# Residual of one pair of sequences transposed by VectorE blocks and transfers instead of TensorE, in a two-layer kernel on one core

## The reference

```python
def _L0_cond_ref(x, ...):
    attn = softmax((x @ Wq) @ (x @ Wk).T * V ** -0.5)          # per sequence
    attn_out = attn @ (x @ Wv) @ Wp + bp
    cms_out = gelu(attn_out @ cW1 + cb1) @ cW2 + cb2 + one_hot(target_codes)
    modifier = gelu(concat([attn_out, cms_out]) @ mW1 + mb1) @ mW2 + mb2
    return clip(x + cms_out + modifier, 0.0, 1.0)

def _L1_cond_ref(stream, hidden_states, W_down, b_down, W_up, b_up, ln_w, ln_b):
    h = gelu(hidden_states @ W_down[stream] + b_down[stream])
    h = h @ W_up[stream] + b_up[stream]
    h = hidden_states + h                                       # the residual
    mean = jnp.mean(h, axis=-1, keepdims=True)
    var = jnp.mean(jnp.square(h - mean), axis=-1, keepdims=True)
    h = (h - mean) * jax.lax.rsqrt(var + LN_EPS)
    return h * ln_w[stream][:, None, :] + ln_b[stream][:, None, :]
```

## Time and profile before

| | |
|---|---|
| median of 3 runs | 1032.73 us (1032.29 to 1033.24) |
| the profiled execution | 1032.2 us, of which span 1030.4 us |
| PE busy | 1023.4 us, 99% of the span, granted clock 0.999 |
| DVE busy | 795.0 us, 77% |
| ACT busy | 524.8 us, 51% |
| POOL busy | 26.5 us, 3% |
| DMA | 103.71 MB, mean 101 GB/s |

### The profile page before, as it was taken

The page is one execution under the profiler, slowest core; times in us unless marked ns, Lnnn a source line. Parts: engine busy times, 40 slices in busy tenths (PEclk is TensorE's granted clock), DMA queues, the critical chain, the costliest instruction groups (busy, mean ns, idle before and its releaser), DMA issues.

```text
span 1030.4 us, 13832 instructions
## 1 busy us (share of the span) xinstructions
PE 1023.4 (99%) x4834; PEld 858.0 (83%) x4834; DVE 795.0 (77%) x1364; ACT 524.8 (51%) x954; POOL 26.5 (3%) x42
## 2 busy tenths in 40 slices
PE   9999999999999999999999999999999999999997
PEld 8899888888888888888889888888888888888886
DVE  5657857767598898887966896677668889887798
ACT  4337864444265443433565587454435644434357
POOL 0000000000000021000000000000000001200001
PEclk9999999999999999999999999999999999999999
DMA  9351311210143272621643312312004322423142
GB/s 209 61 205 39 102 42 49 74 41 21 62 157 118 93 201 86 166 80 54 239 118 109 116 62 82 123 42 82 21 21 163 143 85 100 162 101 107 42 164 82
DMA packets 108558, 103.71 MB, mean 101 GB/s; under 512 B 54254, under 2 KB 89418, under 8 KB 104650
## 3 DMA queue, kind: packets, MB, share of 16 engines
q1 hardware_dynamic: 108400, 102.81, 30.9%
q10 hardware_dynamic: 90, 0.02, 0.0%
HBM read 79.74 MB, written 20.97 MB: 98 GB/s over the span
## 4 chain that ended last, share of the span: by engine, by line
PE 96%; DVE 2%; ACT 1%; issue 0%; DVEq 0%; ACTq 0%
PE bank L231 31%; PE bank L232 31%; PE bank L233 31%; PE bank L270 1%; PE bank L259 1%; DVE z_last L1315 0%; DVE z_last L1326 0%; PE bank L473 0%; PE bank L246 0%; ACT gel L857 0%; DVE xp2l L1043 0%; DVE xp3l L1043 0%; ACT e3h L601 0%; ACT h33h L856 0%; ACT h32h L856 0%
## 5 line engine op out<-in xcount | busy, mean ns | idle before, releaser
L693 ACT ACTIVATE sbc<-sbc,bias 128x512 f32<-128x512 f32 x112 | 80.5, 724 | 234.1 <-DVE sbc L1134 170.0
L231 PE MATMUL bank<-hid_hi,w_lo 128*128 128x512 f32 x512 | 199.7, 390 | 0.0
L233 PE MATMUL bank<-hid_lo,w_hi 128*128 128x512 f32 x512 | 199.3, 389 | 0.0
L232 PE MATMUL bank<-hid_hi,w_hi 128*128 128x512 f32 x512 | 199.2, 389 | 0.0
L1159 DVE TENSOR_TENSOR acc<-bank,acc 128x512 f32<-128x512 f32 x224 | 153.7, 686 | 51.4 <-PE bank L233 51.0
L231 PE MATMUL bank<-ta_hi,w_lo 128*128 128x512 f32 x448 | 174.5, 390 | 0.0
L232 PE MATMUL bank<-ta_hi,w_hi 128*128 128x512 f32 x448 | 174.3, 389 | 0.0
L233 PE MATMUL bank<-ta_lo,w_hi 128*128 128x512 f32 x448 | 174.3, 389 | 0.0
L1134 DVE TENSOR_TENSOR sbc<-bank,sbc 128x512 f32<-128x512 f32 x144 | 97.9, 686 | 41.3 <-PE bank L233 40.9
L1043 DVE TENSOR_TENSOR w_lo<-w_raw,w_hi 128x256 fp32r<-128x256 f32 (+1 forms) x176 | 99.4, 594 | 36.8 <-ACT w_hi L601 36.7
L601 ACT ACTIVATE sbc<-bank 128x512 f32<-128x512 f32 x112 | 66.2, 593 | 114.3 <-PE bank L233 112.4
(11 more groups left out here) (223 smaller groups left out, 1537.8 us busy)
## 6 DMA issues: line engine op xcount, KB each, us to landing
w_raw<-in_L_cond_mW SPq DMA_DIRECT2D x48, 512.0 KB, 3.4
w_raw<-in_L_cond_cW SPq DMA_DIRECT2D x32, 512.0 KB, 4.3
pre_d<-sbc SPq DMA_DIRECT2D x10, 1024.0 KB, 3.9
sbc<-pre_d SPq DMA_DIRECT2D x10, 1024.0 KB, 7.5
x_blk<-in_x SPq DMA_DIRECT2D x64, 64.0 KB, 2.3
e_raw<-in_L_cond_W_down SPq DMA_DIRECT2D x8, 512.0 KB, 4.6
e_raw<-in_L_cond_W_up SPq DMA_DIRECT2D x8, 512.0 KB, 4.1
proj_hi<-aw_hi SPq DMA_DIRECT2D x2, 1024.0 KB, 10.1
```

Source lines behind the costliest of these rows:

```text
L231: nc.tensor.matmul(dst, w_l, a_h, start=start, stop=False, **kw)
L232: nc.tensor.matmul(dst, w_h, a_h, start=False, stop=False, **kw)
L233: return nc.tensor.matmul(dst, w_h, a_l, start=False, stop=stop, **kw)
L693: nc.scalar.activation(dst, dst, ACT.Gelu, **kw).then_inc(g_done[key], 1)
```

## The change

In the norm of pair 1 alone the residual no longer goes through PE. DVE transposes 32x32 blocks of `acc` into `res_blk` (four instructions, after the softmax of pair 2), and sixteen transfers, four after each value tile of pair 2 on ACT's own queue, put the blocks in place in `res`. PE's up-projection starts its banks afresh, and its wait for the values' low parts (`v_l`) moves from the transposes to it. DVE adds bank and `res` into `acc`; mean and sum of squares are taken by ACT from there, with an output nobody reads (`hjunk`), and DVE and POOL do the rest tile by tile instead of half by half. ACT goes on to the value tiles of pair 3 only when all four sums are there. To free semaphores, the transfers of each of the last three column tiles of Wq and Wk share one, so that each waits for both. The branches for probabilities transposed by PE, which no pair used, are removed. The core of the diff:

```diff
-        wq_in, wk_in, wv_in = ([sem(f"w{w}_in{t}") for t in range(KT)] for w in "qkv")
+        wq_in, wv_in = ([sem(f"w{w}_in{t}") for t in range(KT)] for w in "qv")
+        wk_in = [sem("wk_in0")] + wq_in[1:]
...
-                pe.wait_ge(landed[d], 16)
+                pe.wait_ge(landed[d], 32 if i < 2 and d else 16)
...
-                elif n == 1:
-                    pe.wait_ge(v_l, 8 + t + 1)
...
+                if n == 1:
+                    pe.wait_ge(v_l, 8 + t + 1)
...
-                               u_lo[:, s, w], False, True, skip_group_check=True)
+                               u_lo[:, s, w], n == 1 and m == 0, n != 1 or m == MT - 1, skip_group_check=True)
...
-                    token_tile(t)
+                    if n != 1:
+                        token_tile(t)
...
-            v_tiles(0, range(TT))
+            for t in range(TT):
+                v_tiles(0, (t,))
+                if b:
+                    act_move_residual(act, t)
...
                 act_exps(act, n + 1)
+                act_stats_moved(act)
...
+        def act_move_residual(act, q):
+            act.wait_ge(blk_done, 8)
+            grid = lambda tile, quarter: tile[32 * quarter:32 * quarter + 32, :].rearrange("p (x c f) -> p x c f", c=4, f=32)
+            for r in range(4):
+                act.dma_start(grid(res, r)[:, :, q, :], grid(res_blk, q)[:, :, r, :]).then_inc(res_in, 16)
+
+        def act_stats_moved(act):
+            for t in range(TT):
+                col = slice(TT + t, TT + t + 1)
+                act.wait_ge(h_done, t + 1)
+                nc.scalar.activation(hjunk[:, t, :], z_tile(1, t), ACT.Identity, scale=-1.0 / V,
+                                     accum_out=nmean[:, col]).then_inc(nmean_done, 1)
+                act.wait_ge(nmean_done, t + 1)
+                nc.scalar.activation(hjunk[:, t, :], z_tile(1, t), ACT.Square, bias=nmean[:, col],
+                                     accum_out=ssq[:, col]).then_inc(ssq_done, 1)
+            act.wait_ge(ssq_done, TT)
...
+        def dve_residual_blocks(dve):
+            dve.wait_ge(xb_done, 8)
+            for j in range(KT):
+                nc.vector.transpose(res_blk[:, j * TB:(j + 1) * TB], acc[:, j, TB:2 * TB]).then_inc(blk_done, 1)
+
+        def dve_norm_moved(dve):
+            by_feature = lambda tile: tile.rearrange("p (k e) -> p k e", e=P)
+            dve.wait_ge(z_done[0], 4)
+            dve.wait_ge(ln_in[1], 64)
+            dve.wait_ge(res_in, 256)
+            for t in range(TT):
+                dve.wait_ge(up_mm, 4 + t + 1)
+                nc.vector.tensor_tensor(by_feature(z_tile(1, t)), by_feature(ps[t][:, :]),
+                                        res[:, :].rearrange("p (k t e) -> p k t e", k=KT, t=TT)[:, :, t, :], ALU.add)\
+                    .then_inc(h_done, 1)
...
+                dve_residual_blocks(dve)
                 dve_h3(dve, n - 1)
...
-                dve_norm(dve, n - 1)
+                dve_norm_moved(dve)
```

More of the change, by code:

```diff
@@ L361, in pe_values @@
             for t in range(TT):
[L362 to L365, removed]
                 pe.wait_ge(exp_done, 4 * n + t + 1)
@@ L371, in pe_values @@
                 last.then_inc(v_mm, 1)
[L373 to L385, removed]
         def pe_attend(pe, n):
@@ L769, in act_probs_T @@
             for b in range(SEQ):
[L770 to L775 removed]
+                act.wait_ge(raw_in[i], 256 * (n // 2 + 1))
+                act_copy(by_key(pT_hi[i], b), moved(i, b)).then_inc(pT_h, 1)
         def act_ao(act, n):
@@ L1246, in dve_probs_T @@
                 dve.wait_ge(pT_h, 2 * n + b + 1)
-                if n in MOVED:
-                    sub(by_key(pT_lo[i], b), moved(i, b), by_key(pT_hi[i], b)).then_inc(pT_l, 1)
-                else:
-                    sub(pT_lo[i][:, b, :], ps[2 * i + b][:, :], pT_hi[i][:, b, :]).then_inc(pT_l, 1)
+                sub(by_key(pT_lo[i], b), moved(i, b), by_key(pT_hi[i], b)).then_inc(pT_l, 1)
         def dve_blocks_T(dve, n):
@@ L1275, in dve_h3 @@
                 sub(h3[n][1][:, m, :], gel[n][:, m, :], h3[n][0][:, m, :]).then_inc(h3_l, 1)
+        def dve_residual_blocks(dve):
[12 more added lines that the diff above has]
+                    .then_inc(h_done, 1)
+            for t in range(TT):
+                col = slice(TT + t, TT + t + 1)
+                dve.wait_ge(ssq_done, t + 1)
+                nc.vector.tensor_scalar(veps[:, t:t + 1], ssq[:, col], 1.0 / V, LN_EPS, ALU.mult, ALU.add).then_inc(ve_done, 1)
+                nc.vector.scalar_tensor_tensor(out=z_tile(1, t), in0=z_tile(1, t), scalar=nmean[:, col],
+                                               in1=ln_p[1][:, t // TS, 0, :], op0=ALU.add, op1=ALU.mult).then_inc(z_cent, 1)
+                dve.wait_ge(rstd_done, R_BASE[1] + t + 1)
+                dve.wait_ge(z_cent, 4 + t + 1)
+                nc.vector.scalar_tensor_tensor(out=z_tile(1, t), in0=z_tile(1, t), scalar=rstd[:, t:t + 1],
+                                               in1=ln_p[1][:, t // TS, 1, :], op0=ALU.mult, op1=ALU.add)\
+                    .then_inc(z_done[1], 1)
+        R_BASE = (0, 2, 6)
         def dve_norm(dve, n, halves=(0, 1)):
@@ L1304, in dve_norm @@
                         .then_inc(z_done[pp], 1)
-        R_NO = {pt: 4 * NBAT - 3 + c + 1 for c, pt in enumerate(A_STAT)}
+        R_NO = {pt: R_BASE[2] + 1 + c + 1 for c, pt in enumerate(A_STAT)}
         def dve_eps_last(dve, pp, t):
             col = slice(TT * pp + t, TT * pp + t + 1)
-            dve.wait_ge(ssq_done, A_NO[(pp, t)] + 1)
+            dve.wait_ge(ssq_done, TT + A_NO[(pp, t)] + 1)
             nc.vector.tensor_scalar(veps[:, t:t + 1], ssq[:, col], 1.0 / V, LN_EPS, ALU.mult, ALU.add).then_inc(ve_done, 1)
@@ L1682, in pool_program @@
                 if b:
-                    for n in (2 * b - 2, 2 * b - 1):
-                        pool_norm(pool, n, halves)
+                    pool_norm(pool, 2 * b - 2, halves)
+                    pool_norm(pool, 2 * b - 1, singles)
                 pool_s(pool, b)
@@ L1820, in sync_program @@
                 sp.dma_start(proj_lo[:, slot, :], aw_lo[slot][:, :].bitcast(F32)).then_inc(proj_out, 16)
-            for n in MOVED:
-                if n < 2:
-                    move_probs(sp, n)
+            for n in range(2):
+                move_probs(sp, n)
             sync_mlp(sp, 0)
```

31 lines of the change are left out of this document (12 added, 19 removed).

## The result

The changed kernel takes **1038.21 us** in the median of 4 runs (1036.78 to 1039.28), the kernel before 1032.72 us beside it. The ratio is 1.0053, with a 95% interval of 1.0041 to 1.0065: slower by 0.5%, where I had forecast 1032.2 us and given slower a chance of 0.22. The time lies outside the range too.

What follows compares the result with a forecast made beforehand. TensorE was taken as the bound: 1032.2 - 1.67 for removed transposes + 1.18 for a new wait = 1031.7 us profiled; the same -0.5 on the median 1032.73 gave 1032.2. Range 1031.0 to 1035.6.

Steps and rivals of the forecast that it cites:

- The ceiling of 1.67 us: Most the change can gain: TensorE's time for the sixteen residual transposes before the up-projection, 0.16% of the run.
- The issue step: Time from one residual transfer issue to the next on ScalarE's queue: 0.653 us, four in 2.61 us.
- Rival (d): ScalarE's issues take turns with SyncE's sixteen, at 1.31 us each; 1040.4 us, chance 0.05.
- The sum of 238 stays below: From 552 to 560 us, 138 GB/s of load plus 100 for the moves stays below 292, so issues aren't lengthened.
- Rival (c): Issues grow with the runs or are held, steps from 0.83 us; loss above 2 us, chance 0.17.
- D: Microseconds by which ScalarE's queue of sixteen issues ends later than the forecast 562.59 us.
- The chain behind D: A later queue end delays weight pieces, softmax, probabilities and last value tile by the same time.
- my formula: The change in time is -0.5 + D us, the forecast gain of 0.5 less the queue's delay.
- The norm at 1.58 us a tile: VectorE's remaining work in the moved norm, four tiles at 1.58 us from 573.3 to 579.6, taken from the last norm.
- the landed probabilities: SyncE's second move of probabilities, landing at 582.7 us, decides the late chain, with the norm 0.6 us behind.
- The new wait at e = 3: TensorE waits 1.2 us in pair 2's attention, before its fourth feature block, for pair 3's last value remainder.
- The small edits: Block transposes, extra small powers on GpSimd and shared semaphores in the prologue were to cost nothing on TensorE.

Runs made afterwards that it cites:

- c2: The kernel before without TensorE's sixteen transposes of pair 1's residual, nothing in their place and that residual not added; 1030.86 us, ratio 0.9984.
- e1: The changed kernel with SyncE's norm-parameter loads issued behind its moves of pair 2's probabilities, not ahead of them; 1039.34 us, ratio 1.0069.
- x2: x1 with VectorE centering each tile of the moved norm before it finishes the previous tile; 1032.88 us, ratio 1.0004.
- x5: x2 with the weight pieces e1h and e1l split right behind the first value tile, before the residual's transfers; 1031.00 us, ratio 0.9986.
- x4: x3 with the weight pieces e1h and e1l split right behind the first value tile, before the residual's transfers; 1032.26 us, ratio 0.9998.
- x3: x2 with pair 3's last value tile taken ahead of its last probabilities on ScalarE and VectorE, in both batches; 1033.32 us, ratio 1.0008.
- c1: The changed kernel run again with nothing edited, for a second trace; 1038.33 us.
- e2: The changed kernel with the weight pieces e1h and e1l split right behind the first value tile, ahead of most transfer issues; 1036.47 us, ratio 1.0043.
- e3: The kernel before with only the residual's block transposes and ScalarE's sixteen transfers added, their result unread and TensorE's transposes kept; 1036.86 us, ratio 1.0043.
- e4: The changed kernel with 28 useless matmuls on TensorE ahead of its wait for e1l; 1037.88 us, ratio 1.0051.
- e5: The changed kernel with SyncE's move of pair 2's probabilities held back until all sixteen residual transfers have landed; 1043.29 us in one run.
- x1: The changed kernel with pair 1's norm parameters loaded into the first pair's buffer as soon as that pair is stored; 1033.58 us, ratio 1.0010.

## Why the prediction was wrong, point by point

**The ceiling of 1.67 us: right.** c2 gives 1.59 in the median and 1.7 in the span.

**The issue step: right where it is not held.** Four issues take 2.65 us, against my 2.61. A single one takes 0.651 us in the median of e1, the moves with half as many runs 0.611: twice the runs cost 0.04 us. Rival (d), turns with SP, is out: both queues issued at once all along. SP's sixteen took 11.55 us instead of 10.81, not twice as long.

**"The sum of 238 stays below": this is the step that failed.** I asked whether the bandwidth would do, and took a mean of 138 GB/s over 8 us for the load. The question was what stood queued ahead of the first transfer. SP's four parameter loads, 1 MB issued in the 2.4 us before, were in the trace of before, and they are in none of the rows and in no term of the sum. Behind them the first transfer takes 6.5 us to land, and the fifth issue is held until then, 3.05 us instead of 0.65. The sign was there, in the earlier trace rows: an x issue held for 4.4 us. I named it and then left it out of the range, because my price for a hold was the 0.83 us of the earlier trace rows. Rival (c) had the right mechanism, "or is held", and the wrong size: D = 3.2 at the range's end, against 4.15 in the trace.

**The chain behind D: right in kind.** By my formula, -0.5 + 4.15 = 3.65 us. The trace has 4.3. Not all of D is the fifth issue: 0.32 us of it is the late start, and 0.6 the last four issues, which take that long only with the loads and SP's moves together. The piece at 565.5, the softmax, the second move and the attention were late in this order, and PE stopped for e1l as rival (c) had it.

**The norm at 1.58 us a tile: too small.** It took 1.91, 1.3 us more over four tiles. 0.6 us of lag behind the probabilities had been allowed, so 0.7 reach the attention, and 3.65 + 0.7 is 4.35: the span's 4.3. That the two sums agree to 0.1 us is partly luck, since each rests on steps of some tenths. The row came from a norm whose input was a PSUM bank, and x2, which takes the wait for the power away, needs 1.46 us a tile. Of what decides there, the order was wrong too: the norm, not the landed probabilities (DVE works without a gap from 575.04 to 589.94 but for the four waits for the power).

**The new wait at e = 3: not seen in the changed kernel** (0.2 us), since the first block was already late. x2, without holds and slow norm, shows it at 0.8 us; 1.2 had been forecast.

**The small edits.** The four block transposes cost nothing, as forecast. The shared semaphores cost nothing either, as forecast. In the changed kernel PE starts the first tile that waits for two transfers at 8.45 us, 0.29 later than before, but it is 0.28 late already at 6.49, ahead of that wait. In x5 it is the first tile of Wk, which waits for its own transfer alone, that comes late:

```profile
5.20 0.76 PE L260 MATMUL bank<-ident,wk_raw 128*128 128x128 f32 x4 [0.43 <-DMA wk_raw<-in_L_cond_Wk]
```

Such delays differ between traces: ACT's first value tile is 0.1 to 0.8 us later than before in eleven traces with these semaphores, 0.1 in c2 without them, and 0.9 and 1.7 in x4 and x3, whose order in the first batch adds 0.7. What makes them is open.

**What lies beyond the trace.** The median's loss of 5.5 us is 1.2 more than the first trace has. The second trace (c1) has 5.9 in its span: a longer hold, and the half clock reaching DVE's fourth add.

## What to carry to other kernels

Before a DMA issue is put on an engine that has other work, look at what the other queues issued in the few microseconds before it, not at the mean load. Here the first transfer landed only with 1 MB of another queue's loads, and the fifth issue of the queue waited for the first landing, with the engine. Large loads that are not needed soon belong earlier, not where they happened to be harmless. A function that serves both batches changes both, as x3 did. And a duration taken from another place can be off when its operands come from other memories: the power took 0.98 us where 0.54 had been read.

## What the runs showed of the hardware

- An issue on ACT's queue was held in all six traces with 1 MB of SP's loads just in front: 3.05 us (changed), 3.42 (c1), 3.04 (e2), 3.67 (e3), 3.56 (e4) and 3.72 (e5), always the fifth transfer of 64 KB. It ended within 0.2 us of the landing of the queue's first transfer, and so did the fifth issue of 1.1 us in x1. Without the loads in front no issue took over 0.74 us (e1). Which resource the issue waits for no trace shows. The Trainium skill, Perfetto Trace Analysis, section DMA Instruction — HWDGE, has the issue's record run until all its descriptors are generated, and speaks of a descriptor buffer that fills up; a full buffer would fit what is seen here, but was not tested by itself.
- The other statement of the Trainium skill in that section, a generator locked by one sequencer at a time, is not borne out for the length of an issue: in e1 ACT's issues keep 0.651 us in the median while SP's sixteen run beside them in 11.08 us. A lock over a small part of each would not show.
- GpSimd's power takes 0.98 us beside a VectorE operation with two SBUF inputs and 0.54 to 0.56 without.
- TensorE's clock fell to 0.50 after 3.3 us without work (changed), after 3.9 (c1) and after 6.2 (e1); it stayed at 1.00 after 2.3 us (e3) and when 28 filler matmuls stood in the gap (e4). The medians of the changed kernel and e4 are 0.3 us apart, less than the runs can tell; in the changed kernel's second trace the half clock kept DVE's fourth add waiting for 0.67 us.
